# A top-32 window attention: step order rebuilt on all engines, and distance matmuls with 18 rows per head

## The reference, cut to what matters

```python
q = relu(einsum('btd,nde->btne', h, enc_q)); v = relu(einsum('btd,nde->btne', h, enc_v))
for n in range(8):
    diff = q_n[:, idx, :] - q_n[:, :, None, :]          # idx: this token and the 63 before it
    dist = sqrt((diff * diff * metric_n).sum(-1) + 1e-8)
    neg_d, loc = top_k(-where(mask, dist, inf), 32)
    infl = exp(neg_d); infl = infl / (infl.sum(-1) + 1e-8)
    context = einsum('btk,btkd->btd', infl, v_n[top_idx])
    context += (norm(q_n) > 0.2) * 0.1 * (q_n / norm(q_n)) @ (U_n @ V_n)
    outs.append(q_n * context)
x = x + ga * (concat(outs) @ decoder)                    # attention
x = x + gb * (h2 + sum_e gate_e * (h2 @ A_e.T) @ B_e.T)  # experts, h2 = layernorm(x) scaled
```

## Time and profile before

| | us |
|---|---|
| median of 3 executions | 915.0 (914.45 to 927.3) |
| span of the profiled execution (all its time between first and last instruction) | 940.7 |
| TensorE matmul busy | 838.5 |
| VectorE busy | 802.6 |
| ScalarE busy | 627.9 |
| GpSimd busy | 465.8 |
| mean granted TensorE clock | 0.832 |

### The profile page before, as it was taken

One profiled execution on the slowest core, in us unless ns is written; L12 is line 12 of the kernel. 1 busy time (PEld: TensorE's weight loads), 2 busy tenths in 40 slices (PEclk: granted clock), 3 DMA queues, 4 the chain that ended last, 5 costly groups with the idle time before them and its releaser, 6 DMA issues.

```text
span 940.7 us, 25723 instructions
## 1 busy us (share of the span) xinstructions
PE 838.5 (89%) x4437; PEld 672.4 (71%) x4437; DVE 802.6 (85%) x6746; ACT 627.9 (67%) x1862; POOL 465.8 (50%) x871
## 2 busy tenths in 40 slices
PE   5978899999999999999979799999999897988865
PEld 3446678777877778777868677787778676767654
DVE  6956998879899887878989898879788898989990
ACT  4962467666677666666768686666666786767763
POOL 2124355545556555545555564555455564646542
PEclk9977877777789777777989997777777999999965
DMA  5300000000000000000000000000000000000000
GB/s 169 91 8 24 14 22 20 25 28 21 24 25 27 27 25 20 24 26 21 24 25 27 28 27 26 26 21 24 25 19 27 25 27 26 28 26 28 26 9 9
DMA packets 49225, 26.95 MB, mean 29 GB/s; under 512 B 5512, under 2 KB 48592, under 8 KB 49104
## 3 DMA queue, kind: packets, MB, share of 16 engines
q1 hardware_dynamic: 49104, 25.90, 9.3%
HBM read 10.28 MB, written 4.19 MB: 15 GB/s over the span
## 4 chain that ended last, share of the span: by engine, by line
DVE 36%; PE 34%; issue 16%; ACT 6%; POOL 4%; DMA 2%; DVEq 0%; POOLq 0%; ACTq 0%; SPq 0%
DVE work L946 19%; DVE m L936 12%; PE psD L1114 10%; PE psC L1159 6%; PE psW L1175 4%; PE psD L1111 3%; PE psW L1186 3%; PE psW L1177 2%; ACT key L649 2%; ACT big L661 2%; PE psX L1166 2%; DMA big<-in_x 1%; PE psX L1167 1%; DVE key L758 1%; POOL big L478 1%
## 5 line engine op out<-in xcount | busy, mean ns | idle before, releaser
L946 DVE MATCH_REPLACE8 work<-m,work 128x64 f32<-128x64 f32 x1536 | 300.9, 205 | 0.0
L1114 PE MATMUL psD<-sst,tst 128*128 128x224 f32 x1024 | 270.5, 392 | 0.0
L1114 PEld LDWEIGHTS psD<-sst,tst 128*128 128x128 f32 x1024 | 225.5, 221 | 25.9 <-issue 8.5
L936 DVE MAX8 m<-work 128x8 f32<-128x64 f32 x1536 | 210.8, 208 | 0.0
L478 POOL TENSOR_TENSOR big<-work,con 128x512 f32<-128x512 f32 x128 | 162.5, 1290 | 47.7 <-ACT work L624 47.7
L457 POOL TENSOR_TENSOR hsc<-gat,rnn 128x8 f32<-128x8 f32 x64 | 13.0, 204 | 271.2 <-ACT rnn L706 271.2
L1159 PE MATMUL psC<-vst,big 128*128 128x34 f32 x1024 | 132.7, 287 | 13.7 <-ACT big L661 11.6
L1159 PEld LDWEIGHTS psC<-vst,big 128*128 128x128 f32 x1024 | 126.6, 201 | 24.6 <-issue 22.3
L946 DVE MATCH_VALUE_LOAD work<-m,work 128x8 f32 x1536 | 115.8, 75 | 0.0
L1111 PE MATMUL psD<-mask_bf,ident_bf 128*128 128x448 bf16 x256 | 106.3, 415 | 3.5 <-DVE key L962 3.5
L946 DVE MATCH_REPLACE8 work<-m,key 128x64 f32<-128x64 f32 x512 | 100.4, 205 | 0.0
(11 more groups left out here) (199 smaller groups left out, 1506.6 us busy)
## 6 DMA issues: line engine op xcount, KB each, us to landing
hst<-hT_all SPq DMA_DIRECT2D x64, 96.0 KB
tst<-qT_all SPq DMA_DIRECT2D x256, 17.0 KB
big<-in_x SPq DMA_DIRECT2D x16, 256.0 KB, 2.7
tst<-nst SPq DMA_DIRECT2D x256, 1.0 KB
xs<-in_x SPq DMA_DIRECT2D x64, 64.0 KB, 1.8
out<-yo SPq DMA_DIRECT2D x64, 64.0 KB, 1.6
sst<-nst SPq DMA_DIRECT2D x128, 3.0 KB
con<-in_consts SPq DMA_DIRECT2D x1, 549.5 KB, 5.6
```

The source lines that it names most:

```text
L936: last = v.max(m8[:, h], src[:, h * WIN:(h + 1) * WIN])
L946: last = v.match_replace(work[:, s, cols], m8[:, h], src[:, cols], GONE)
L1114: last = mm(bank_of(r)[:, g, 0:SW], tst[:, s, r, g], sst[:, s, g], start=False, stop=(g == NG - 1), skip_group_check=True)
```

## The change

The distance matmuls use only the rows of one r (16 query rows and two rows of norms, `tst[rows]`, `sst[rows]`), so that neighbours in the code lie on different rows of the array; all four masks come first. tst loses its padded copies and the memset of them. The transpose of osp moves from the end of step k+1 to step k+2. The orders of all engines are written anew; on top of the diff below:

- **SyncE**: the load of xs is first.
- **GpSimd**: gat and n2g; sqs; wun; sst; t1 with rden and osp (i-2); hsc, t1, t2, t2 (now i-1: they wait for cst of the same step); selm last.
- **ScalarE**: weights(0), weights(1); h2T; lnn, rnn; to_wts(0); the two relu of key; yo; qh; to_wts(1); oT; the two cst copies; x2; Ln of key; lv_c, nm_c, rs_c, nb_c (i-2); vst; Exp of key; n_c (now i-2); n2, nst.

```diff
@@ -149,7 +149,7 @@
...
-        tst = sb("tst", [P, 2, NR, NG, CH])
+        tst = sb("tst", [P, 2, NG, CH])
...
@@ -373,6 +373,10 @@
...
             def step(i, ph):
+                k = i + 1
+                if there(i, 1):
+                    need(sync, att_ready, k - 3)
+                    sync.dma_start(xs[:, (ph + 1) % 4], xc[:, bass.ds(k, 1)].squeeze(1)).then_inc(xs_in[(ph + 1) % 4], 16)
                 k = i - 3
...
                     for r in range(NR):
                         rows = slice(32 * r, 32 * r + HD + 1)
-                        sync.dma_start(tst[rows, s, r], qT_all[rows, :, bass.ds(c0 + WIN, CH)]).then_inc(rows_in[s], 16)
+                        sync.dma_start(tst[rows, s], qT_all[rows, :, bass.ds(c0 + WIN, CH)]).then_inc(rows_in[s], 16)
                     sync.wait_ge(nst_ready, k + 1)
...
                     for r in range(NR):
-                        sync.dma_start(tst[32 * r + HD + 1:32 * r + HD + 2, s, r], nst[NG * r:NG * (r + 1), s, WIN:3 * WIN]).then_inc(rows_in[s], 16)
-                k = i + 1
-                if there(i, 1):
-                    need(sync, att_ready, k - 3)
-                    sync.dma_start(xs[:, (ph + 1) % 4], xc[:, bass.ds(k, 1)].squeeze(1)).then_inc(xs_in[(ph + 1) % 4], 16)
+                        sync.dma_start(tst[32 * r + HD + 1:32 * r + HD + 2, s], nst[NG * r:NG * (r + 1), s, WIN:3 * WIN]).then_inc(rows_in[s], 16)
...
@@ -952,42 +965,37 @@
...
-                if there(i, 0):
                     rounds(i, ph, 1)
+                    rounds(i, ph, 2)
 
                 k, s = i + 1, (ph + 1) % 2
                 if there(i, 1):
                     dve.wait_ge(qhs_ready, k + 1)
                     e = key[:, s].rearrange("p (h j) -> p h j", h=NH)
                     v.scalar_tensor_tensor(out=e, in0=pH[:, :, WIN:2 * WIN], scalar=0.0, in1=e, op0=ALU.max, op1=ALU.min).then_inc(d2_ready, 1)
-                if there(i, 0):
-                    rounds(i, ph, 2)
 
                 if there(i, -2):
                     dve.wait_ge(x2_ready, i - 1)
                     v.bn_stats(st_c[:], x2[:, ph % 2]).then_inc(stc_ready, 1)
-
-                def between():
-                    if there(i, -2):
-                        wait_alone(dve, stc_ready, i - 1)
-                        wait_alone(dve, nc_ready, i - 3)
-                        v.bn_aggr(mv_c[:, ph % 2], st_c[:]).then_inc(mvc_ready, 1)
-                    if there(i, -1):
-                        s = (ph - 1) % 2
-                        dve.wait_ge(cst_ready, 2 * i)
-                        need(dve, rden_ready, i - 2)
-                        v.tensor_scalar(den[:, s], cst[:, s, :, HD], 1e-8, None, ALU.add).then_inc(den_done, 1)
-
-                def late():
+                k, s = i - 1, (ph - 1) % 2
+                if there(i, -1):
+                    dve.wait_ge(cst_ready, 2 * (k + 1))
+                    need(dve, rden_ready, k - 1)
+                    v.tensor_scalar(den[:, s], cst[:, s, :, HD], 1e-8, None, ALU.add).then_inc(den_done, 1)
+                if there(i, -2):
+                    wait_alone(dve, stc_ready, i - 1)
+                    wait_alone(dve, nc_ready, i - 3)
+                    v.bn_aggr(mv_c[:, ph % 2], st_c[:]).then_inc(mvc_ready, 1)
+
+                def reciprocals():
                     if there(i, -1):
                         dve.wait_ge(den_done, i)
                         v.reciprocal(rden[:, (ph - 1) % 2], den[:, (ph - 1) % 2]).then_inc(rden_ready, 1)
 
                 if there(i, 0):
-                    rounds(i, ph, 3, between, late)
+                    rounds(i, ph, 3, reciprocals)
                 else:
-                    between()
-                    late()
+                    reciprocals()
...
@@ -1106,13 +1114,19 @@
             def bank_of(r):
                 return psD[:, r].rearrange("p (g x) -> p g x", g=NG)
 
-            def distances(s, r):
-
-                mm(bank_of(r)[:, :, 0:SW], ident_bf[:], mask_bf[:].unsqueeze(1).broadcast_to([P, NG, SW]), start=True,
-                   stop=False, skip_group_check=True)
+            def window_masks():
+
+                for r in range(NR):
+                    mm(bank_of(r)[:, :, 0:SW], ident_bf[:], mask_bf[:].unsqueeze(1).broadcast_to([P, NG, SW]), start=True,
+                       stop=False, skip_group_check=True)
+
+            def distances(s):
+
                 for g in range(NG):
-                    last = mm(bank_of(r)[:, g, 0:SW], tst[:, s, r, g], sst[:, s, g], start=False, stop=(g == NG - 1),
-                              skip_group_check=True)
+                    for r in range(NR):
+                        rows = slice(32 * r, 32 * r + HD + 2)
+                        last = mm(bank_of(r)[:, g, 0:SW], tst[rows, s, g], sst[rows, s, g], start=False,
+                                  stop=(g == NG - 1), skip_group_check=True)
                 return last
 
             def step(i, ph):
@@ -1130,41 +1144,62 @@
                             nc.tensor.transpose(psW[:, w, (h % 4) * P:(h % 4 + 1) * P], wun[:, s, h],
                                                 ident).then_inc(wt_ready, 1)
 
-                weights_T(0)
-
-                s, x4 = ph % 2, (ph - 2) % 4
-                if there(i, -2):
-                    k = i - 2
-                    pe.wait_ge(xs_in[x4], 16 * (k // 4) + 16)
-                    pe.wait_ge(oT_ready, k + 1)
-                    mm(pAtt, ident, xs[:, x4], start=True, stop=False)
-                    mm(pAtt, oT[:, s], dec_b[:, bass.ds(k // CPB, 1)].squeeze(1), start=False, stop=True).then_inc(att_ready, 1)
-                weights_T(1)
+                def contexts(half):
+
+                    k, s, s4 = i - 1, (ph - 1) % 2, (ph - 1) % 4
+                    if there(i, -1):
+                        if half == 0:
+                            if isinstance(i, int) and i == 1:
+                                pe.wait_ge(gb_ready, 2)
+                            need(pe, cst_ready, 2 * k)
+                            pe.wait_ge(vst_ready, k + 1)
+                        pe.wait_ge(wts_ready, 2 * k + 1 + half)
+                        for h in range(4 * half, 4 * half + 4):
+                            last = mm(pC[:, h * 2 * VD:(h + 1) * 2 * VD], wts[:, s, h],
+                                      vst[:, s4, h].rearrange("p v e -> p (v e)"), start=True, stop=True)
+                        if half == 1:
+                            last.then_inc(c_ready, 1)
 
                 k, s = i - 3, (ph - 3) % 2
                 if there(i, -3):
                     pe.wait_ge(nc_ready, k + 1)
-                    need(pe, x2_ready, min(k + 2, NCH) if isinstance(k, int) else k + 2)
                     nc.tensor.transpose(pN2, n_c[:, s], ident).then_inc(pn2_ready, 1)
 
-                k, s, s4 = i - 1, (ph - 1) % 2, (ph - 1) % 4
-                if there(i, -1):
-                    if isinstance(i, int) and i == 1:
-                        pe.wait_ge(gb_ready, 2)
-                    need(pe, cst_ready, 2 * k)
-                    pe.wait_ge(vst_ready, k + 1)
-                    for h in range(NH):
-                        if h % 4 == 0:
-                            pe.wait_ge(wts_ready, 2 * k + 1 + h // 4)
-                        last = mm(pC[:, h * 2 * VD:(h + 1) * 2 * VD], wts[:, s, h],
-                                  vst[:, s4, h].rearrange("p v e -> p (v e)"), start=True, stop=True)
-                    last.then_inc(c_ready, 1)
+                weights_T(0)
 
                 k, s = i - 3, (ph - 3) % 2
                 if there(i, -3):
                     pe.wait_ge(h2T_ready, k + 1)
                     mm(pY, ident, x2[:, s], start=True, stop=False)
                     mm(pY, h2T[:, s], g_b[:, bass.ds(k // CPB, 1)].squeeze(1), start=False, stop=True).then_inc(y_ready, 1)
+
+                weights_T(1)
+
+                contexts(0)
+
+                k, s = i - 2, ph % 2
+                if there(i, -2):
+                    pe.wait_ge(osp_ready, k + 1)
+                    need(pe, yo_ready, k)
+                    nc.tensor.transpose(pO, osp[:, s], ident).then_inc(po_ready, 1)
+
+                contexts(1)
+
+                k, s, x4 = i - 2, ph % 2, (ph - 2) % 4
+                if there(i, -2):
+                    pe.wait_ge(xs_in[x4], 16 * (k // 4) + 16)
+                    pe.wait_ge(oT_ready, k + 1)
+                    mm(pAtt, ident, xs[:, x4], start=True, stop=False)
+                    mm(pAtt, oT[:, s], dec_b[:, bass.ds(k // CPB, 1)].squeeze(1), start=False, stop=True).then_inc(att_ready, 1)
+
+                k, s = i + 2, (ph + 2) % 2
+                if there(i, 2):
+                    pe.wait_ge(rows_in[s], ROWS_IN * (k // 2) + ROWS_IN)
+                    need(pe, vst_ready, k)
+                    need(pe, wts_ready, 2 * (k - 2))
+                    for v in range(2):
+                        last = mm(pV[:, v], hst[:, s, v * WIN:(v + 2) * WIN], encv_sb[:], start=True, stop=True)
```

(63 more changed lines are left out.)

161 lines of the change are left out of this document (74 added, 87 removed).

## The result

The changed kernel takes **948.5 us** (median; 944.0 to 952.5, 4 executions) against 916.7 us (914.5 to 927.3, 4) for the kernel before on the same chip: ratio 1.031 [1.023, 1.040], **slower**. The forecast was 960 us. Executions of the kernel before spread widely (906 to 962 us over all chips used, with medians of 938 to 943 us in the later measurements), so ratios here compare like executions only, those close to the shortest of each kernel, and where the median of all executions of before is given it is called the plain median. Measured once more in experiment 5, the changed kernel takes 948.1 us beside a plain median of 938.7 us, which is 1.0% more: how large the loss is depends on which executions of before it is held against.

A forecast was written before the change was run, and what follows sets the result against it. VectorE was taken to bound short steps, TensorE at a low clock the long ones. A 10.6 us loop plus 2.5 for half clock gives 13.1; 127 + 825 for 63 steps + 7 for turns = 960 us, range 888 to 1010.

The forecast's parts named there:

- A: The forecast's own case: 63 steps of 12.8 to 13.68 us, 941 to 997 us in all; chance 0.50.
- The distances: 16 packed passes on TensorE: 1.95 instead of 3.0 us per step at full clock, priced like the contexts; lower bound 0.76.
- 9.5 + 2.5 = 12.0 us: Loop through TensorE if the packed passes took only 0.8 us: 127 + 756 + 22 for turns = 905 us.
- One fall in every step: TensorE's clock falls once per step behind contexts or att, 6.7 us at half clock, costing 2.5 us more.
- VectorE keeps its instructions: VectorE's work stays the same, only the distance minimum moves behind the third of four rounds; no cost in the sum.
- pN waits for selm, idle 1.3 us: TensorE idles 1.3 us per step ahead of pN until GpSimd's selm, now last there; part of the 10.6 us loop.
- VectorE waiting for x2 in nearly all steps: Sign in the profile after: VectorE waits for qh or x2 in nearly all steps.
- key_ready hidden: About 3 us for the key behind the minimum, against 3.1 us of VectorE work: just hidden at full clock.
- The osp wait worth little: TensorE's 38.0 us of waits for the osp transpose go, but are worth little by themselves.
- Loop turns at 7 us: 13 hardware loop turns cost VectorE 2.2 us each, less 1.65 us of slack: 7 us in all.
- D: Rival: the 18-row passes don't run side by side, loop 14.2 us, 1022 us in all; chance 0.12.
- C: Rival: TensorE is never the bound, the 50.6 us qh wait goes, 890 us as floor; chance 0.15.

The follow-up runs named there:

- Experiments 3 and 4: Changed kernel with selm issued right behind sst on GpSimd: 954.8 us; changed kernel with the value matmuls issued three times: 925.7 us.
- experiment 2: Changed kernel's new order on all engines, but distance matmuls with all 128 rows as before: 1049.8 us, ratio 1.143.
- experiments 1 and 6: Kernel before with only the distances packed, osp transpose ahead of all distance passes: 936.8 us; the same with that transpose behind them: 930.7 us.
- experiment 9: Changed kernel with bn_aggr, den and reciprocal back inside VectorE's fourth round and ScalarE's Exp ahead of lv_c: 953.3 us, ratio 1.038.
- experiment 10: Changed kernel with bn_aggr, den, reciprocal back inside the fourth round, Exp ahead of lv_c, and value matmuls three times: 907.0 us.
- experiment 8: Changed kernel with bn_stats reading a constant tile instead of waiting for x2, and the x2 copy behind Exp: 944.4 us.

## Why the prediction was right, and where its steps were not

**The result**: 948.5 us lies in A's own range of 941 to 997 and 11.5 us from the forecast of 960. The core of the reasoning held: TensorE's work goes down, its clock goes down further, and the long steps belong to a loop through TensorE that hides behind VectorE at full clock and not at half clock. Experiments 3 and 4 tell this cause from the order of selm: earlier selm gives nothing, more matmuls give 23 us. That the number came out so close is in part luck, since errors of opposite sign met in it. The forecast was one step of 13.1 us, 63 times; measured are 50 steps without a turn, 29 of them under 11.8 us and the others up to 14.7, and 13 steps with a turn, of 14.4 to 17.3 us. Their mean is 13.01 us, and 12.46 without the time of the turns. And the loop is another one: forecast from one end of the distances to the next, 10.6 us at full clock, measured from fourth round to fourth round, where the chain to x2 takes 10.19 us and VectorE's small work follows.

**The distances** were the term of the sum that was mis-sized: 0.98 us and 1.80 us instead of 1.95 and 3.6, near the lower bound of 0.76. In experiment 2 the same 16 passes with all 128 rows take 104.99 - 101.97 = 3.0 us at full clock, so the 3.0 was right. The contexts were the wrong nearest row: there every pass loads a new tile for all rows, here neighbours on other rows overlap, loads included. The argument that only two neighbours can run side by side failed as well. By the Trainium skill, "TensorE: Matmul & The Clock Gate", Part 3, four row tiles gain 3.07 times; the trace agrees, 3.0 / 0.98 = 3.06, at 224 columns and in fp32. "TensorEngine Tiling (Array Packing)", Key Properties, has the engine drain when the tiling changes; here the four masks and the hand-over to the 18-row passes take 576.63 - 575.79 = 0.84 us, where the forecast had 0.76 without any, so by this estimate that change is worth 0.1 us at most.

With that size my own text had the loop at 9.5 + 2.5 = 12.0 us and 905 us in all. It came out at 948 because other terms were off in the other direction: the loop turns (35 us instead of that case's 22), VectorE's small work (16 us instead of nothing), and what the half clock costs, with steps of 13.0 and, where it lasts, 14.4 to 14.7 us instead of 12.0.

**One fall in every step** was wrong in form. The clock falls less often than before, 28 times, and then stays at 0.50 for up to 54 us. The prediction named this only as what could go wrong ("that it never rose again"). The masks and distances that I took for what lifts the clock had become 1.8 us long instead of 3.8. That packing lowers the clock without the new order is shown by experiments 1 and 6.

**"VectorE keeps its instructions" cost nothing** in the sum; it cost 0.25 us a step, 16 us. The instructions are the same, but bn_aggr and den stand bare between minimum and fourth round, each waiting for the one before it, instead of inside a round. By itself undoing this gives nothing (experiment 9); with a higher clock it gives 18.7 us (experiment 10 against 4). So it is a cost only where VectorE is the bound.

**pN waits for selm, idle 1.3 us**: right in place and size (1.27 us at 574.57 in one step, 57.1 us in 61), wrong as the path that sets the step: that is the chain to bn_stats, through contexts and cst (experiment 8). **VectorE waiting for x2 in nearly all steps**: in 28 of 63. **key_ready hidden**: right, no such wait appears. **The osp wait worth little**: right (experiment 6). **Loop turns at 7 us** were too low: VectorE loses 32.5 + 2.6 us there. The forecast had 1.65 us of each turn vanish in a wait for TensorE. But in 11 of the 13 steps with a turn x2 was there 1.4 to 3.6 us ahead of bn_stats (584.46 against 587.87): VectorE is the bound there and the turn adds its whole length.

**Rivals**: D's 1022 us was the price of distances that don't overlap; experiment 2 is that case and has 1049.8. C's floor of 890 us has been reached by no version; the best median is 907.

## What to carry to other kernels

Before you make TensorE faster, ask who waits for it: here nobody waited for it at full clock, and with the shorter matmuls the granted clock went from 0.83 to about 0.7. If the granted clock falls when work is removed, repeat some matmuls whose results are written anyway and time a few amounts; three times gave 17 to 46 us in the packed kernels here, five times took 17 back, and in the kernel before there was no gain over its better executions. Small dependent instructions cost less here inside a long run of their engine (11.25 against 11.71 us per short step), and a reordered step has to be priced together with the edit that comes with it: the two did not add.

## What was unexpected of the hardware

Sixteen passes with 18 rows each, neighbours on different rows of the array, took 0.98 us at full clock, weight loads included, against 3.0 us for sixteen with 128 rows (1.80 us at half clock). The granted clock can stand at 0.50 over 54.4 us in which TensorE is busy for 51.8 by its records (109.60 to 164.00), so a high busy share is no sign of a high clock. More work raised the clock only up to a point: in the kernel of experiment 10, 12 value passes per step had 0.860 to 0.878 and 20 had 0.872 to 0.884. And in the order of before packing moved it from 0.83 to 0.72. What exactly of TensorE's activity is counted stays open.
